# Attention stage: the pi weights of four batches on a block diagonal, spread by six products of 376 columns instead of 24 of 94

## The chip, the cores and the metric

The kernel runs on one core of a Trainium2 chip. The metric is the time of one execution in microseconds (us) as the device measures it. The engines are named as the profile names them: PE is TensorE's matmul side and PEld its weight loads, DVE is VectorE, ACT is ScalarE, POOL is GpSimd and SP is SyncE, which here only issues DMAs.

## The reference, cut to what matters

64 batches of 93 tokens (16 image patches and 77 text tokens) with 192 features go through an embedding, one attention stage and one feed-forward stage. The change is in the attention stage:

```python
w = (x @ w_qkv).reshape(b, n, h, -1).transpose(0, 2, 1, 3)        # 12 heads of 64
w_normed = w / maximum(norm over n, 1e-12)
logits = sum(w_normed * w_normed, -1) * temp
Pi = softmax(logits, axis=-1)                                      # over the 93 tokens
Pi_norm = Pi / (sum(Pi, -1) + 1e-08)
dots = einsum('bhn,bhnd->bhd', Pi_norm, w * w)[:, :, None, :]
out = -(w * Pi[..., None]) * (1 / (1 + dots))
return out.transpose(0, 2, 1, 3).reshape(b, n, -1) @ w_out + b_out
```

Everything is float32 here. For each batch and each head there is one row Pi of 93 weights. Each has to stand beside all 64 rows of its head before it can be multiplied with w, which lies with the 768 head features on the partitions.

## The kernel before, in words

The kernel has three stages. The first (to about 150 us) makes the embeddings. The second is the attention, together with the feed-forward's routing: layer norm, codes z, scores, the top four of 64 in each of eight groups, gates. The third, from about 750 us, is a long pipeline of small experts over 12 tiles.

The second stage works on 16 units of `UB` = 4 batches (372 tokens). It is a software pipeline written out by hand: in pass `i` (`pass_pe`, `pass_dve`, `pass_act`, `pass_pool`, `pass_sp`) each engine does a part of unit `a = i` (layer norm, w, squares, norms, logits, softmax), of unit `b = i - 1` (pi spread, attention, output product, residual) and of unit `g = i - 2` (second layer norm, codes, scores, gates). Each engine has one queue and runs it in the order in which those functions call; semaphores join the engines.

The softmax leaves `pi`, 128 partitions x 94: partition `32 b + h` holds batch b and head h, columns 0 to 92 the weights and column 93 the reciprocal of their sum (`pi_complete`, L1178). To spread it, `spread_pi(u, c)` (L1460 to L1469) does, for each of the `CH` = 6 chunks of 128 head features, one product per batch: the weights `headsel[:, b, c]` (128x128, ones where partition 32 b + h belongs to a feature's head) times the whole of `pi`, which gives 94 columns. The four results stand side by side in one PSUM bank of `pair0`. On DVE, `w_pi` (L1183, L1186) multiplies w with the 4 x 93 columns and copies the four scales out; on POOL, `w2_pi` (L716) multiplies with w again, and `attn_dots` (L1190) sums on DVE.

What stands around it in a pass, in the order of the queues:
- PE: `spread_pi` 0 and 1; the six transposes of unit a's normed tokens (L1413); `spread_pi` 2 and 3; six transposes of unit g (L1413 again); `spread_pi` 4 and 5; `z_product` (L1441); `w_product` 0 to 5 (L1426) with `scores` (L1449) between; the output products (L1487); `logits` (L1456); gate transposes (L1475). The two banks of `pair0` are shared: chunk c of a spread waits until `w_pi(c-2)` has read its bank (`s_rsc`).
- DVE, at the end of a pass: `logits_max` (L1220, L1222), `pi_recip` (L1162), `pi_made` (L1166), `pi_sum` (L1170), `pi_sum_eps` (L1174), `pi_complete` (L1178), the norm of the next unit (L1119), the residual (L1229, L1232), `bn_stats` (L1106). At the start of the next: `w_pi` 0, `bn_aggr` (L1112), `w_pi` 1, the norm of unit g (L1119), `w_pi` 2, 3, `attn_dots` 0, 1, `w_pi` 4, 5, `attn_dots` 2 to 5, `neg_attn` (L1197 to L1201), and then the eight-fold max and the marking of the gates (`top8` L1128, `mark` L1139).
- ACT: `logits_exp` (L901), then the gate copies 1 and 2 (L913), and in the next pass the copies of the transposed tokens (L865), w (L871), squares with a sum (L873, 93 columns each) and scores (L897).
- POOL: `rstd` (L689, L691), `w2_pi`, the shifts and products of the gates (L704, L710), `attended` (L724).

Constants are set in stage 1: `headsel` is cleared by DVE (L1009) and its ones are placed by POOL in four steps (L669); `lsel` is cleared by POOL between the stages (L683).

Of the kernel before, what the change touches and what calls it, by code (L numbers as in the profile page):

```python
# [28 lines left out]
AX = mybir.AxisListType  # L29
# [6 lines left out]
N = NI + NT  # L36
# [10 lines left out]
CH = INNER // 128  # L47
UB = 4
# [48 lines left out]
def wait(eng, sem, value):  # L97

    if isinstance(value, int) and value <= 0:
        return  # L100
    eng.wait_ge(sem, value)
# [42 lines left out]
def build(nc, t):  # L144

    with ExitStack() as ctx:
        def sem(name):
            return ctx.enter_context(nc.semaphore(name))
# [20 lines left out]
        class Carver:  # L169
# [4 lines left out]
            def __call__(self, rows, shape, dt=F32):  # L174
# [7 lines left out]
                if len(shape) > 1:  # L182
# [7 lines left out]
        pair0, pair1 = ring[:, 0:2], ring[:, 2:4]  # L190
# [43 lines left out]
        cl = Carver(LATE)  # L234
# [4 lines left out]
        bout = cl(ST, [D])  # L239
        tempc = cl(128, [1])  # L240
        maskh = cl(128, [CH, HEADS])
        headsel = cl(128, [UB, CH, 128])
        pz = cl(DH2, [2, 128])
        cbd = cl(128, [E])

# [1 line left out]
        c2 = Carver(0, LATE)  # L247
# [21 lines left out]
        pe_ = c2(128, [N])  # L269
        psm = c2(128, [1])  # L270
        prc = c2(128, [1])
        pi = c2(128, [N + 1])
        pss = c2(128, [1])
        pse = c2(128, [1])
        rsc = c2(128, [CH, UB])
# [42 lines left out]
        s_zero = sem("constants_zeroed")  # L318
# [16 lines left out]
        s_c2 = sem("attention_constants")  # L335
# [14 lines left out]
        s_pr, s_pi, s_ps, s_pse, s_pix = (sem("pi_recip"), sem("pi_made"), sem("pi_sum"), sem("pi_sum_eps"),  # L350
                                          sem("pi_complete"))
        s_pb = sem("pi_spread")
        s_wpi, s_rsc = sem("w_pi"), sem("pi_scale_copied")
        s_w2pi = sem("w2_pi")
        s_dt, s_ds, s_dm, s_na = sem("dots_summed"), sem("dots_scaled"), sem("dots_negated"), sem("neg_attn")
# [71 lines left out]
        def stage1_over(eng):  # L427

            eng.wait_ge(s_todma[0], 64 * 6)
            eng.wait_ge(s_todma[1], 64 * 5)  # L430
            eng.wait_ge(s_idma[0], 16 * 4)
            eng.wait_ge(s_idma[1], 16 * 4)
            eng.wait_ge(s_ws, 2)
            eng.wait_ge(s_bc, 1)
            eng.wait_ge(s_w2c, 1)

        def has(u):

            return not isinstance(u, int) or 0 <= u < UNITS
# [189 lines left out]
        def _(pool):  # L629
            p_ = nc.gpsimd  # L630
# [34 lines left out]
            text_rstd(1)  # L665
            gather(3, 1)
            for b in range(UB):
                v = headsel[:, b].rearrange("p c (o d) -> p c o d", o=2)
                p_.affine_select(out=v, in_=v, compare_op=ALU.not_equal, fill=1.0, base=-32 * b,  # L669
                                 pattern=[[-2, CH], [-1, 2], [0, DH]], channel_multiplier=1).then_inc(s_c2, 1)  # L670
            text_rstd(2)
# [9 lines left out]

            stage1_over(pool)
            p_.memset(lsel, 0.0)  # L683
            p_.memset(mh2, -0.5).then_inc(s_c2, 1)
            pool.wait_ge(s_c2, 7)

# [119 lines left out]
        def _(act):  # L806
            a_ = nc.scalar
# [91 lines left out]
            def logits_exp(u):  # L899
                act.wait_ge(s_lm, u + 1)  # L900
                a_.activation(pe_, lg, ACT.Exp, bias=nmax, accum_out=psm).then_inc(s_pe, 1)  # L901

            def scores_exp(u, s):
                act.wait_ge(s_sd, SUB * u + s + 1)
                wait(act, s_gu, SUB * u)
                a_.activation(se[:, s], sd[:, s], ACT.Exp).then_inc(s_se, 1)
# [9 lines left out]
            def pass_act(i):  # L916
                a, g = i, i - 2
                if has(a):
                    copy_xT("A", a)
                if has(g):  # L920
                    copy_xT("G", g)
                if has(g):
                    z_copies(g)
                for c in range(CH):
                    if has(a):
                        w_copy(a, c)
                    if has(g):
                        if c < SUB:
                            scores_copy(g, c)
                        if c == 1:  # L930
                            z_part2(g)
                            scores_exp(g, 0)
                        if c == 4:
                            scores_exp(g, 1)
                if has(g - 1):
                    copy_bias(g - 1)
                if has(g):
                    scores_exp(g, 2)
                    gates_copy(g, 0)
                if has(a):  # L940
                    logits_exp(a)
                if has(g):
                    gates_copy(g, 1)
                    gates_copy(g, 2)
# [58 lines left out]
        def _(dve):  # L1003
# [3 lines left out]
            v_.memset(cbd, 0.0)  # L1007
            v_.memset(maskh, 1.0)
            v_.memset(headsel, 0.0)  # L1009
            v_.memset(b2p[:], 0.0)  # L1010
            v_.memset(w2p[:], 0.0).then_inc(s_zero, 1)
            dve.wait_ge(s_const, 1)
# [82 lines left out]


            stage1_over(dve)
            v_.memset(sc[:, :, :, M:M + 8], SENTINEL)
            v_.memset(v4, SENTINEL).then_inc(s_c2d, 1)
            dve.wait_ge(s_c2, 7)  # L1100
# [62 lines left out]

            def pi_made(u):
                dve.wait_ge(s_pr, u + 1)
                v_.tensor_scalar(pi[:, 0:N], pe_, prc, None, ALU.mult).then_inc(s_pi, 1)  # L1166

            def pi_sum(u):
                dve.wait_ge(s_pi, u + 1)
                v_.tensor_reduce(pss, pi[:, 0:N], AX.X, ALU.add).then_inc(s_ps, 1)  # L1170

            def pi_sum_eps(u):
                dve.wait_ge(s_ps, u + 1)
# [1 line left out]

            def pi_complete(u):
                dve.wait_ge(s_pse, u + 1)
                v_.reciprocal(pi[:, N:N + 1], pse).then_inc(s_pix, 1)  # L1178

            def w_pi(u, c):  # L1180
                dve.wait_ge(s_pb, CH * u + c + 1)
# [52 lines left out]
            def pass_dve(i):  # L1234
                a, b, g = i, i - 1, i - 2
                if has(b):
                    w_pi(b, 0)
                if has(g):
                    bn_aggr("G", g)
                if has(b):  # L1240
                    w_pi(b, 1)
                if has(g):
                    for s in range(SUB):
                        norm("G", g, h1, s)
                if has(g) and not has(b):
                    v_.memset(zst[96:ZROWS], 1.0).then_inc(s_ones, 1)
                if has(b):
                    w_pi(b, 2)
                    w_pi(b, 3)
                    attn_dots(b, 0)  # L1250
                    attn_dots(b, 1)
                    w_pi(b, 4)
                    w_pi(b, 5)
                    for c in range(2, CH):
                        attn_dots(b, c)
                    neg_attn(b)

                if has(g):
                    top8(g, 0)
                    top4(g, 0)  # L1260
                    mark(g, 0)
                    top8(g, 1)
                    top4(g, 1)
                    raw(g, 0)
                    mark(g, 1)
                    raw_sum(g, 0)
                    top8(g, 2)
                    raw_recip(g, 0)
                    top4(g, 2)
                    raw(g, 1)  # L1270
                    mark(g, 2)
                if has(a):
                    norms_floored(a)
                if has(g):
                    raw_sum(g, 1)
                if has(a):
                    norms_inverted(a)
                if has(g):
                    raw_recip(g, 1)
                if has(a):  # L1280
                    head_weights(a)
                if has(g):
                    raw(g, 2)
                if has(a + 1):
                    dve.wait_ge(s_x0, 16 * (a + 2))
                    bn_stats("A", a + 1, x0)
                if has(g):
                    raw_sum(g, 2)
                if has(a + 1):
                    bn_aggr("A", a + 1)  # L1290
                if has(g):
                    raw_recip(g, 2)
                if has(a):
                    logits_max(a)
                if has(a):
                    pi_recip(a)
                    pi_made(a)
                    pi_sum(a)
                    pi_sum_eps(a)
                    pi_complete(a)  # L1300
                if has(a + 1):
                    for s in range(SUB):
                        norm("A", a + 1, x0, s)
                if has(b):
                    residual(b, 0)
                    residual(b, 1)
                if has(b):
                    dve.wait_ge(s_h1, b + 1)
                    bn_stats("G", b, h1)
# [60 lines left out]
        def _(pe):  # L1370
# [88 lines left out]

            def spread_pi(u, c):  # L1460
                pe.wait_ge(s_pix, u + 1)
                if c < 2:
                    pe.wait_ge(s_wsq, CH * u + 5 + c)
                else:
                    wait(pe, s_rsc, CH * u + c - 1)
                for b in range(UB):
                    last = t_.matmul(pair0[:, c % 2, (N + 1) * b:(N + 1) * (b + 1)], headsel[:, b, c],  # L1467
                                     pi, start=True, stop=True)
                last.then_inc(s_pb, 1)  # L1469

            def gates_transposed(u, s):
                pe.wait_ge(s_z1, u + 1)
# [218 lines left out]
```

## Time and profile before

| | us |
|---|---|
| median of three runs | 1595.14 |
| lowest and highest | 1578.29 and 1599.72 |
| the profiled execution, whole | 1585.62 |
| its span, first to last instruction | 1583.9 |
| the stretch of 14 passes of stage 2 (208.8 to 704.5 us) | 495.7 |
| mean granted TensorE clock of the span | 0.933 |

The granted clock is a share of 2.4 GHz; 0.50 is the lower level, 1.2 GHz. A row of a timeline gives start, duration, engine, line, operation, shapes, count, and in brackets the idle time of the engine before it with what ended it. A float32 product shows as two MATMUL instructions and two LDWEIGHTS, so a spread of one chunk is 8 of each.

### The profile page before, as it was taken

To read this page: it belongs to the slowest core of one execution; us is meant where nothing else is said; L and a number is where in the kernel's file an instruction comes from. 1 tells how busy PE (TensorE), PEld (TensorE's weight loads), DVE (VectorE), ACT (ScalarE), POOL (GpSimd) and SP (SyncE) were. 2 spreads that over 40 slices of the span, in tenths; PEclk is the share of its full clock that TensorE was granted. 3 is DMA by queue.
4 is the path that set the end of the run, shared out by engine and by line. 5 is a ranking of instruction groups with operands and counts; after the bars stand their busy time and mean duration, and the time that the engine had idled before them with its cause. 6 is when DMAs were issued, how large, how long until landed. Compare 5 with 4: busy or idle time off the path is not lost.

```text
span 1583.9 us, 29744 instructions
## 1 busy us (share of the span) xinstructions
PE 1408.5 (89%) x8184; PEld 644.7 (41%) x8184; DVE 1183.5 (75%) x3446; ACT 1031.2 (65%) x2119; POOL 1048.1 (66%) x770
## 2 busy tenths in 40 slices
PE   4971789989999998986699999999999999999997
PEld 2630567766666666764122222222222222222222
DVE  4573278887888978877678877777787787778874
ACT  0231344444544544432599999999999899999995
POOL 3650266566666766655487787877878778787775
PEclk9955799999999989987699999999999999999998
DMA  8436311121211211113311413214132131321310
GB/s 245 117 97 89 49 30 54 55 63 56 80 53 53 65 53 53 56 48 103 88 37 43 90 34 70 55 42 89 28 76 55 42 76 40 78 55 42 74 38 13
DMA packets 93351, 102.28 MB, mean 65 GB/s; under 512 B 12215, under 2 KB 90575, under 8 KB 93007
## 3 DMA queue, kind: packets, MB, share of 16 engines
q1 hardware_dynamic: 89945, 96.01, 24.8%
q0 software_dynamic: 2112, 3.79, 0.9%
q10 hardware_dynamic: 1232, 1.84, 0.4%
q14 instruction: 45, 0.37, 0.1%
q8 instruction: 17, 0.28, 0.1%
HBM read 64.83 MB, written 33.52 MB: 62 GB/s over the span
## 4 chain that ended last, share of the span: by engine, by line
issue 40%; PE 19%; DVE 18%; POOL 13%; DMA 4%; ACT 3%; SPq 1%; POOLq 1%; DVEq 0%; ACTq 0%
POOL arena L783 10%; DVE arena L1139 4%; PE ring L1456 3%; DVE arena L1128 3%; DMA arena<-h_scratch 3%; PE ring L1467 2%; DVE arena L1119 2%; PE ring L1426 2%; PE ring L1569 2%; PE code L1582 2%; PE ring L1441 2%; DVE arena L1214 1%; PE ring L1375 1%; DVE arena L1154 1%; PE ring L1384 1%
## 5 line engine op out<-in xcount | busy, mean ns | idle before, releaser
L1336 DVE TENSOR_TENSOR arena<-ring,arena 128x496 f32<-128x496 f32 x1008 | 614.0, 668 | 178.3 <-ACT ring L974 134.9
L783 POOL TENSOR_TENSOR arena<-arena 128x992 f32<-128x992 f32 x264 | 603.7, 2298 | 178.3 <-ACT arena L974 167.9
L1569 PE MATMUL ring<-arena,w_stack 99*128 99x496 bf16 x1536 | 401.9, 379 | 16.2 <-DVE arena L1336 15.4
L974 ACT ACTIVATE ring<-ring 128x992 f32<-128x992 f32 x396 | 385.1, 987 | 34.9 <-PE ring L1569 32.5
L1582 PE MATMUL code<-arena,w_pad 128*32 128x496 f32 x3072 | 398.7, 592 | 1.5 <-ACT arena L979 0.6
L1569 PEld LDWEIGHTS ring<-arena,w_stack 99*128 99x128 bf16 x1536 | 119.4, 97 | 450.0 <-DVE arena L1336 257.0
L974 ACT ACTIVATE arena<-ring 128x992 f32<-128x992 f32 x252 | 251.3, 997 | 11.0 <-PE ring L1569 3.1
L1426 PE MATMUL ring<-arena 96*128 96x372 f32 x384 | 145.0, 510 | 5.7 <-ACT arena L873 4.4
L1582 PEld LDWEIGHTS code<-arena,w_pad 128*32 128x32 f32 x3072 | 61.1, 108 | 138.4 <-issue 115.5
L969 ACT ACTIVATE ring<-ring 128x496 f32<-128x496 f32 x216 | 112.7, 568 | 6.1 <-PE ring L1569 4.8
L1467 PE MATMUL ring<-arena 128*128 128x94 f32 x768 | 105.0, 296 | 9.1 <-DVE arena L1178 7.6
L716 POOL TENSOR_TENSOR arena<-arena 128x372 f32<-128x372 f32 x96 | 91.8, 974 | 31.8 <-DVE arena L1183 31.4
L865 ACT COPY arena<-ring 96x744 f32<-96x744 f32 x32 | 24.8, 775 | 132.9 <-PE ring L1413 132.9
L1467 PEld LDWEIGHTS ring<-arena 128*128 128x128 f32 x768 | 100.7, 211 | 13.2 <-DVE arena L1178 8.2
L1426 PEld LDWEIGHTS ring<-arena 96*128 96x128 f32 x384 | 73.9, 200 | 76.9 <-issue 28.4
L873 ACT ACTIVATE arena<-ring 128x93 f32<-128x93 f32 x384 | 92.5, 280 | 0.0
L710 POOL TENSOR_TENSOR arena<-arena 124x512 f32<-124x512 f32 x48 | 58.6, 1221 | 50.6 <-DVE arena L1158 49.4
L1413 PE MATMUL ring<-ident,arena 124*96 124x124 f32 x192 | 31.4, 308 | 64.9 <-DVE arena L1119 64.9
L689 POOL TENSOR_SCALAR arena<-arena 124x3 f32<-124x3 f32 x32 | 7.5, 234 | 121.9 <-DVE arena L1112 121.9
L873 ACT ACTIVATION_READ_ACCUMULATOR arena<-ring 128x1 f32 x384 | 86.4, 238 | 0.0
L724 POOL TENSOR_TENSOR arena<-arena 128x372 f32<-128x372 f32 x96 | 77.9, 832 | 8.7 <-DVE arena L1201 8.7
L1139 DVE MATCH_REPLACE8 arena<-arena 124x72 f32<-124x72 f32 x384 | 78.4, 217 | 0.0
(126 smaller groups left out, 1737.1 us busy)
## 6 DMA issues: line engine op xcount, KB each, us to landing
arena<-gates SPq DMA_DIRECT2D x48, 496.0 KB, 6.7
gates<-arena SPq DMA_DIRECT2D x16, 744.0 KB, 10.0
arena<-h_scratch SPq DMA_DIRECT2D x32, 279.0 KB
arena<-z_parts SPq DMA_DIRECT2D x144, 62.0 KB, 2.2
h_scratch<-arena SPq DMA_DIRECT2D x16, 279.0 KB
z_parts<-arena SPq DMA_DIRECT2D x48, 93.0 KB, 1.7
arena<-h_scratch SPq DMA_DIRECT2D x12, 372.0 KB
out_h<-arena SPq DMA_DIRECT2D x12, 372.0 KB
```

The source lines that it names most:

```text
L716: p_.tensor_tensor(w2pi[:, c], wpi[:, c], wv[:, c], ALU.mult).then_inc(s_w2pi, 1)
L724: p_.tensor_tensor(o, o, natt[:, c].unsqueeze(2).to_broadcast([128, UB, N]), ALU.mult).then_inc(s_o, 1)
L783: p_.tensor_tensor(gated[:, quad % SPACES, j:j + 2], hid[:, POOL_DUOS.index(duo) % 2], gst[:, block // EB, j:j + 2], ALU.mult).then_inc(s_ ...
L873: last = a_.activation(wsq[:, c, N * b:N * b + N], src[:, N * b:N * b + N], ACT.Square, accum_out=n2[:, c, b:b + 1])
L969: last = a_.activation(product if to_pool is None else to_pool[:, k], product, ACT.Gelu_apprx_tanh)
L974: a_.activation(product if to_pool is None else to_pool, product, ACT.Gelu_apprx_tanh).then_inc(s_hid, 1)
L1139: last = v_.match_replace(mr[:, s, g], v4[:, s, g], sc[:, s, g], CHOSEN)
L1336: v_.tensor_tensor(gated[:, quad % SPACES, j + p], duo_bank(duo, p), gst[:, block // EB, j + p], ALU.mult).then_inc(s_gat, 1)
L1426: mm = t_.matmul(o, wq[:, h, 128 * c:128 * c + 128], xT["A"][:, h], start=(h == 0), stop=(h == 1))
L1467: last = t_.matmul(pair0[:, c % 2, (N + 1) * b:(N + 1) * (b + 1)], headsel[:, b, c], pi, start=True, stop=True)
L1569: mm = t_.matmul(duo_bank(duo, p), w1s[:, x:x + 128], zst[:, o, j + p], start=True, stop=True)
L1582: mm = t_.matmul(code_bank[32 * j:32 * j + 32, 0:TN], w2p[:, chunk(2 * j + o, eb, k)], gated[:, quad % SPACES, j], start=(quad == 0), stop ...
```

## The change

`headsel` loses its batch index: one 128x128 selector per chunk serves all four batches, with ones for every partition 32 b + h of the head. In exchange pi gets a block-diagonal form: `pis`, 128 x 4 x 94, holds batch b's rows in column block b and zeros elsewhere. One product of 376 columns per chunk then gives what four of 94 gave. New work per unit: ACT copies four blocks of 32 partitions x 93 from `pi` to `pis` (`pi_placed`), behind `logits_exp` and ahead of gate copies 1 and 2; DVE writes the four scale columns with one small multiply (`pi_scale_placed`), behind `pi_complete` and ahead of the next unit's norm. PE waits for both.

```diff
-        headsel = cl(128, [UB, CH, 128])
+        headsel = cl(128, [CH, 128])
+        unitsel = cl(128, [UB])
...
-        pi = c2(128, [N + 1])
+        pi = c2(128, [N])
+        pis = c2(128, [UB, N + 1])
+        prs = c2(128, [1])
...
             for b in range(UB):
-                v = headsel[:, b].rearrange("p c (o d) -> p c o d", o=2)
+                v = headsel.rearrange("p c (o d) -> p c o d", o=2)
+                if b > 0:
+                    pool.wait_ge(s_c2, 2 + b)
                 p_.affine_select(out=v, in_=v, compare_op=ALU.not_equal, fill=1.0, base=-32 * b,
...
             p_.memset(lsel, 0.0)
+            p_.memset(pis, 0.0)
...
+            def pi_placed(u):
+                act.wait_ge(s_pi, u + 1)
+                wait(act, s_pb, CH * u)
+                for b in range(UB):
+                    rows = slice(32 * b, 32 * b + 32)
+                    last = a_.copy(pis[rows, b, 0:N], pi[rows])
+                last.then_inc(s_pip, 1)
...
                     logits_exp(a)
+                    pi_placed(a)
...
+            v_.memset(unitsel, 0.0)
...
+            dve.wait_ge(s_zero, 1)
+            for b in range(UB):
+                v_.memset(unitsel[32 * b:32 * b + 32, b:b + 1], 1.0)
...
             def pi_made(u):
                 dve.wait_ge(s_pr, u + 1)
-                v_.tensor_scalar(pi[:, 0:N], pe_, prc, None, ALU.mult).then_inc(s_pi, 1)
+                wait(dve, s_pip, u)
+                v_.tensor_scalar(pi, pe_, prc, None, ALU.mult).then_inc(s_pi, 1)
...
-                v_.reciprocal(pi[:, N:N + 1], pse).then_inc(s_pix, 1)
+                v_.reciprocal(prs, pse).then_inc(s_prs, 1)
+
+            def pi_scale_placed(u):
+                dve.wait_ge(s_prs, u + 1)
+                wait(dve, s_pb, CH * u)
+                v_.tensor_scalar(pis[:, :, N], unitsel, prs, None, ALU.mult).then_inc(s_pix, 1)
...
                     pi_complete(a)
+                    pi_scale_placed(a)
...
             def spread_pi(u, c):
                 pe.wait_ge(s_pix, u + 1)
+                pe.wait_ge(s_pip, u + 1)
...
-                for b in range(UB):
-                    last = t_.matmul(pair0[:, c % 2, (N + 1) * b:(N + 1) * (b + 1)], headsel[:, b, c],
-                                     pi, start=True, stop=True)
-                last.then_inc(s_pb, 1)
+                t_.matmul(pair0[:, c % 2, 0:UB * (N + 1)], headsel[:, c], pis.rearrange("p b n -> p (b n)"),
+                          start=True, stop=True).then_inc(s_pb, 1)
```

## Rows read from the trace of the kernel before

**Rows 1.** The page: the span, TensorE's clock in 40 slices, the spread's two groups.
```profile
span 1583.9 us, 29744 instructions
PEclk9955799999999989987699999999999999999998
L1467 PE MATMUL ring<-arena 128*128 128x94 f32 x768 | 105.0, 296 | 9.1 <-DVE arena L1178 7.6
```
**Rows 2.** Stretches of PE, PEld, DVE, ACT, POOL busy time, clock, DMA share, GB/s.
```profile
208.80:704.50 495.70, 448.87 (x2757) 335.10 (x2758) 413.63 (x1927) 225.28 (x991) 315.52 (x348) 0.95 0.18 57
526.30:559.70 33.40, 30.38 (x199) 22.74 (x200) 29.45 (x139) 16.19 (x71) 22.65 (x26) 1.00 0.20 63
...
276.10:311.10 35.00, 31.96 (x199) 24.31 (x200) 29.58 (x139) 16.19 (x71) 22.73 (x26) 0.95 0.20 61
...
665.50:704.50 39.00, 35.41 (x199) 26.29 (x200) 29.23 (x133) 16.19 (x71) 22.73 (x26) 0.87 0.15 47
```
**Rows 3.** The chain of waits in a warm pass (start, us, what).
```profile
528.20 0.17 DVE arena L1174
528.38 0.04 DVE arena L1178
...
528.47 0.13 DVE arena L1119
...
536.34 1.76 PE ring L1467 x16
538.10 1.28 PE ring L1441 x4
```
**Rows 4.** The timeline of the same pass on PE, DVE and ACT.
```profile
526.91 0.37 ACT L901 ACTIVATE arena<-arena 128x93 f32<-128x93 f32 x1 [5.30 <-DVE arena L1222]
...
529.03 1.93 PE L1467 MATMUL ring<-arena 128*128 128x94 f32 x16
529.23 0.57 ACT L913 COPY arena<-ring 128x496 f32<-128x496 f32 x1 [1.40 <-PE ring L1475]
...
530.99 0.53 DVE L1183 TENSOR_TENSOR arena<-arena,ring 128x372 f32<-128x372 f32 x1
531.65 2.02 PE L1467 MATMUL ring<-arena 128*128 128x94 f32 x16
...
532.15 0.15 DVE L1186 COPY arena<-ring 128x4 f32<-128x4 f32 x1
...
535.50 0.84 PE L1413 MATMUL ring<-ident,arena 124*96 124x124 f32 x6 [1.83 <-DVE arena L1119]
...
542.72 1.11 DVE L1128 MAX8 arena<-arena 124x8 f32<-124x64 f32 x8 [0.75 <-ACT arena L897]
```
**Rows 5.** The chain in a pass with a fallen clock.
```profile
568.89 1.48 PE ring L1413 x6
570.37 3.37 PE ring L1467 x16
573.73 2.54 PE ring L1441 x4
```
**Rows 6.** Busy time in a pause of PE and right behind it.
```profile
566.60:568.80 2.20, 0.46 (x5) 0.29 (x3) 2.13 (x4) 0.00 (x0) 1.83 (x2) 0.93 0.23 49
568.90:578.80 9.90, 9.90 (x31) 7.62 (x32) 5.56 (x17) 1.61 (x3) 5.29 (x6) 0.50 0.41 141
```
**Rows 7.** Small ACT activates on 93 columns, from the page.
```profile
L873 ACT ACTIVATE arena<-ring 128x93 f32<-128x93 f32 x384 | 92.5, 280 | 0.0
```
**Rows 8.** Clearing and waiting at the start of stages 1 and 2.
```profile
2.30 2.62 DVE L1009 MEMSET arena<- 128x3072 f32 x1 [0.59 <-issue]
16.89 2.72 DVE L1016 TENSOR_SCALAR arena<-arena 2x4928 int32<-2x4928 int32 x1 [7.55 <-DMA arena<-in_beta]
...
134.53 0.74 POOL L683 MEMSET arena<- 128x768 f32 x1 [7.40 <-DMA h_scratch<-arena]
151.17 0.88 DVE L1106 BATCH_NORM_STATS2 arena<-arena 124x6 f32<-124x192 f32 x3 [16.17 <-DMA arena<-h_scratch]
```

More of the change, by code:

```diff
@@ L352, in build @@
         s_pb = sem("pi_spread")
+        s_prs, s_pip = sem("pi_sum_recip"), sem("pi_placed")
         s_wpi, s_rsc = sem("w_pi"), sem("pi_scale_copied")
@@ L1165, in pi_made @@
                 dve.wait_ge(s_pr, u + 1)
-                v_.tensor_scalar(pi[:, 0:N], pe_, prc, None, ALU.mult).then_inc(s_pi, 1)
+                wait(dve, s_pip, u)
+                v_.tensor_scalar(pi, pe_, prc, None, ALU.mult).then_inc(s_pi, 1)
             def pi_sum(u):
                 dve.wait_ge(s_pi, u + 1)
-                v_.tensor_reduce(pss, pi[:, 0:N], AX.X, ALU.add).then_inc(s_ps, 1)
+                v_.tensor_reduce(pss, pi, AX.X, ALU.add).then_inc(s_ps, 1)
             def pi_sum_eps(u):
```

## The prediction

> **What bounds the kernel now.** The page comes first: its row of the spread's products says 105 us of PE time in 768 instructions, all in stage 2, and its clock row shows full speed in stage 3 and dips in stage 2 [rows 1]. Stage 3 is not touched by the edit, so I looked no further there. Stage 1 sees only the constants. The question is one pass of stage 2, 16 times.
>
> Then busy time by pass. A pass without a dip of the clock lasts 33.4 us; of 14 passes seven have a mean clock below 1 and last 35.0 to 39.0 us; the 14 together take 495.7, that is 28.1 more than 14 times 33.4, or 4.0 for each of the seven [rows 2]. No engine is full in a warm pass: PE is busy 30.4 of 33.4 us and DVE 29.5. The pass is a loop of dependences, so the chain of waits is read next. It goes: logits on PE, softmax on DVE, norm and residual on DVE, norm of unit g, its transposes on PE, then the spreads of chunks 4 and 5 (1.76 us), z (1.28 us), w, the scores' copy, DVE's eight-fold max and marking, and again logits [rows 3]. So of a unit's six spreads only the last pair lies on the chain. The first two pairs lie beside DVE work: PE has spread pair 0 and 1 from 529.03 on, for 1.93 us, while `w_pi(0)` starts at 530.99 straight behind other DVE work with no idle time; and behind pair 2 and 3 PE stands idle for 1.83 us until DVE has normed unit g [rows 4].
>
> **The change part by part.**
>
> *The spread products.* A pair of chunks is 16 instructions of 94 columns now, and 4 of 376 columns afterwards. The nearest row is z, 4 instructions of 372 columns with 128-wide weights: 1.28 us warm. 376 columns make it 1.29. In the chain the pair of spreads costs 1.76 [rows 3], so the gain is 0.47 us in a warm pass. With the clock at its lower level a pair costs 3.37 and z 2.54, a gain of about 0.8 [rows 5]. Three of the 16 passes show it wholly at that level, as these rows do: 3 x 0.8 + 13 x 0.47 = 8.5 us. Pairs 0, 1 and 2, 3 become shorter by as much, at no gain: the first is covered by DVE's residual and statistics, the second ends in the pause. Only unit 0 has no such cover; I count 1 us there. Together 9.5 us. Bounds: nothing (0) if the wait only moves, and 1.93 - 1.29 = 0.64 by the timeline's length of the pair, 16 x 0.64 = 10 plus the cold extra, about 12.
>
> What comes next in the way: DVE stands idle 0.75 us for the scores before the first max [rows 4]. A gain of 0.47 fits in it, so DVE does not swallow it.
>
> *One rule on weights.* In this trace z's 4 full-width weight loads are hidden below its products, since the four take just 1.28 us [rows 3]; I take the new pair the same way. The Trainium skill, "TensorE: Matmul & The Clock Gate", section "Part 3: Packing small matmuls", says that a weight load overlaps running matmuls only if it goes to other row groups. By that rule the full-height loads of the selector would stand beside the products, and the pair would gain next to nothing; z's row does not agree with it.
>
> *The scale column on DVE.* `pi_complete` is on the chain with 0.04 us only, since the norm behind it does not wait for it: from 528.38 to the norm at 528.47 is 0.09 us. Now a second instruction waits for its result and stands before the norm. A dependent pair of such small instructions is 0.18 us apart (528.20 to 528.38) [rows 3], and behind it comes the same 0.09: the norm starts 0.18 to 0.20 us later. Everything DVE does up to the norm of unit g is in order behind it, so the chain pays in full: 16 x 0.19 = 3.0 us. Bounds 0 (never seen better than its issue) and 0.3 a pass, 5 us.
>
> *The four copies on ACT.* No row shows a copy of 32 partitions. The nearest are activates of 128x93: 280 ns each [rows 7], and logits_exp itself 0.37 [rows 4]. Four: 0.65 us if they overlap as in L873, whose 384 activates take 92.5 us busy or 0.24 each plus their tails; 1.5 us at 0.37 each. I take 1.0. They start when `pi_made` is done, 527.9, and end at 528.9, about when PE is ready for the spreads (529.03). A lateness is free up to the slack: the first spread is then done at 528.9 + 0.7 = 529.6, while `w_pi(0)` does not start before 530.99 [rows 4], so 1.3 us are free. Queued behind them on ACT are the gate copies 1 and 2. Copy 1 moves from 527.28 to 528.9; PE's next transposes into that bank come at about 530.3. Copy 2 waits for PE until 529.23 anyway [rows 4] and moves to about 529.5; SP's store of the gates follows it by as much, and z's wait for it is 8 us off. Cost 0; if the copies took 0.65 each, 2.6, it would still be below 3.
>
> *The added waits.* DVE's `pi_made` waits for copies of a unit ago, ACT and DVE for spreads of a unit ago: long done. PE's wait for `s_pip` is the one above. 0.
>
> *Constants.* Clearing the selector takes DVE 2.62 us for 3072 columns, afterwards a quarter; DVE then idles 7.55 us for DMAs, so the gain is hidden. The new clearing of `pis`, 376 columns, is half of L683's 0.74 us, and four small DVE fills cost less than 0.74 together; both lie in the 16.17 us in which DVE waits for the first tokens [rows 8]. POOL's four selector steps already run one after another. 0.
>
> Sum at an unchanged clock: -9.5 + 3.0 = -6.5 us.
>
> **TensorE's clock.** In the seven passes the clock drops from 2.4 to 1.2 GHz in or right behind the pause of PE before unit g's transposes: in 566.6 to 568.8 PE is busy for 0.46 of 2.2 us, and the 9.9 us behind it run at 0.50 [rows 6]. It falls in about half of the passes, with a pause of 1.83 us [rows 4]. The change lengthens this pause: spread 3 may start when `w_pi(1)`'s copy has ended, 532.30 + 0.19, and lasts 0.64, so PE is through at 533.1; the transposes start at 535.7. The pause becomes 2.5 us, and before spread 2 there is a new one of 0.7, as the tokens' transposes are done at 531.1 and spread 2 waits for DVE until 531.8. I expect more falls, 11 of 14 to 16. Against that the stretch behind the pause is now made of long products throughout, half as long in time, so each fall should cost less: between 1.6 (the 35.0 us pass) and 4.0 [rows 2], I take 2.9. 11 x 2.9 = 32, against 28 now: +4 to +5 us. Bounds: no fall at all, -28; 15 falls at 5 us, +47.
>
> Sum: -6.5 + 4.5 = -2 us. Against the profiled execution, 1585.62, this gives 1583.6. That execution lies 9.5 us below the median of the three runs shown, which spread by 21 us. Their mean is 1591.0, the median 1595.1. As the forecast is for a median of a few runs, I put it in between: **1588 us**. A difference of under 2% (32 us) counts as no change here.
>
> **Rivals.**
> - *The clock turns against it.* Place: the pause before unit g's transposes. It decides once nearly all passes fall and a fall is no cheaper than now: 15 x 4.0 = 60, +32; with -6.5 that is +25, 1613 us against the runs. For it: the pause of 1.83 grows to 2.5. Against: the products behind are dense. At 5 us per fall, as in the 39.0 us pass, it is 15 x 5 - 28 - 6.5 = +40: 1628, beyond 2%. Chance 0.15, of this 0.05 for the latter.
> - *The clock turns for it.* As many falls as now but each at 1.6 us, 7 x 1.6 - 28 = -17, with -6.5 gives 1565; none at all gives -34.5, 1554. For it: the shorter recovery. Against: a longer pause. Chance 0.15, of this 0.04 for none.
> - *The copies are late.* If an ACT copy of 32 partitions costs 1 us instead of 0.25, the spread starts 3 us later and DVE waits 1.8 a pass for it: 16 x 1.8 = +29 - 6.5, 1611. No row has such a cost. Chance 0.04.
> - *The product gains nothing.* If the weight loads are not hidden, four times the 0.11 us at which the 16 follow one another (1.76 / 16) come on top of 1.29, 1.73 in all, the old value. Then only the DVE cost stays: +3 + 4.5, 1595. It is what the page's rule above would do. Chance 0.04.
> - *Forecast*: a near wash, 1588, its own range 1572 to 1604. Chance 0.62.
>
> **How the numbers follow.** Beyond 2% faster (below 1556): only the case without any fall, 0.04. Beyond 2% slower (over 1620): 0.05 from the first rival, 0.01 from late copies. The rest, 0.90, is within 2%. The range 1566 to 1611 takes the forecast's own, nearly all of the first two rivals' milder halves and the fourth; what lies outside is about 2 in 10.
>
> **What the profile of the changed kernel would show.** The pair of chunks 4 and 5 in the chain with 4 instructions of 1.3 us in a warm pass; right wherever DVE's wait before the first max shrinks from 0.75 to about 0.5. The norm behind the scale column 0.2 us later after L1178's successor. A warm pass of 33.1 us instead of 33.4. PE idle 2.5 us before unit g's transposes, and more passes with a mean clock below 1. ACT's four copies over before the gate transposes end. I would be wrong if a warm pass is not shorter, if DVE waits for the first spread, or if passes with a dip become fewer.

## The result: 1.5% slower, and the profile after

Before, the median of four runs was 1589.51 us (1578.29 to 1599.72); with the change it is 1615.14 us (1609.02 to 1626.94). The ratio is 1.0146, interval [1.0098, 1.0195]. I had forecast 1588 us with a range to 1611. The time lies outside the range, by a cause that stands nowhere in my prediction. A ratio, here and below, leaves out the executions in the slow state, which take over 1.5% longer than the fastest one of their kernel.

The profiled executions differ by the same 25.6 us: spans 1583.9 and 1609.5 us. The page of the changed kernel first: the span, TensorE's clock in 40 slices, the spread's products (columns as in [rows 1]), and the instruction queue q14 with packets, MB and share. Its packets come where DVE's program needs them, at its branches above all, so it is read as DVE's.

```profile
span 1609.5 us, 28796 instructions
PEclk9855799999999998996799999999999999999998
q14 instruction: 45, 0.37, 0.1%
L1495 PE MATMUL ring<-arena 128*128 128x376 f32 x192 | 85.2, 572 | 17.1 <-DVE arena L1205 8.4
```

The spread did what the edit says: 192 instructions in 85.2 us in place of 768 in 105.0. Yet the kernel is longer. The first reading that helps is to cut both spans into the same five stretches, by the same landmarks (the first logits of stage 2, the end of its last pass, the tiles' first instructions in stage 3):

| us | before | after | difference |
|---|---|---|---|
| start, stage 1 included | 171.3 | 175.0 | +3.7 |
| stage 2, 15 passes | 530.0 | 524.3 | -5.7 |
| transition | 144.2 | 147.1 | +2.9 |
| stage 3, 11 steps from tile to tile | 723.1 | 747.7 | +24.6 |
| end | 15.4 | 15.4 | 0 |

Stage 2, where the edit is, became shorter. All but 1 us of the loss is in stage 3, whose code the edit does not touch. Next, stage 3 by tile: busy time of PE, PEld, DVE, ACT, POOL, clock, DMA share and GB/s of two tiles in a row, before

```profile
910.90:978.40 67.50, 65.15 (x396) 16.39 (x395) 52.37 (x88) 61.66 (x78) 51.47 (x23) 1.00 0.25 57
978.40:1043.90 65.50, 64.70 (x396) 16.34 (x394) 51.87 (x86) 61.50 (x78) 51.46 (x23) 1.00 0.27 58
```

and after:

```profile
911.90:985.70 73.80, 67.58 (x396) 16.65 (x395) 52.40 (x88) 61.61 (x78) 51.48 (x23) 0.95 0.23 52
985.70:1051.20 65.50, 64.66 (x396) 16.33 (x394) 51.83 (x86) 61.47 (x78) 51.48 (x23) 1.00 0.26 58
```

Tiles go in pairs, as DVE's loop holds two. One tile of a pair takes 65.5 us in both kernels. The other takes 67.5 before and 73.8 after, at a clock of 0.95. Four pairs are so, the last is not: a loop of five turns is branched back in four times. 4 x 6.3 = 25 us is the whole difference of stage 3. The work in the two tiles is the same (396 products, 78 on ACT).

What DVE does in the long tile: its timeline around the branch (start, duration, what, in brackets the idle time before it and what ended it), before

```profile
968.17 1.26 DVE L1336 TENSOR_TENSOR arena<-ring,arena 128x496 f32<-128x496 f32 x2 [0.55 <-ACT ring L974]
971.64 7.24 DVE L1336 TENSOR_TENSOR arena<-ring,arena 128x496 f32<-128x496 f32 x12 [2.21 <-issue]
```

and after, with PE's timeline beside it:

```profile
969.12 1.26 DVE L1364 TENSOR_TENSOR arena<-ring,arena 128x496 f32<-128x496 f32 x2 [0.55 <-ACT ring L991]
976.66 3.58 DVE L1364 TENSOR_TENSOR arena<-ring,arena 128x496 f32<-128x496 f32 x6 [6.28 <-issue]
...
977.39 0.59 PE L1596 MATMUL ring<-arena,w_stack 99*128 99x496 bf16 x1 [5.45 <-DVE arena L1364]
977.92 1.88 PE L1609 MATMUL code<-arena,w_pad 128*32 128x496 f32 x8
...
984.22 1.04 PE L1609 MATMUL code<-arena,w_pad 128*32 128x496 f32 x8
```

In both kernels DVE stands still behind the branch, and it waits for no other engine: the releaser is "issue". Before it is 2.21 us, after 6.28 us. PE waits 5.45 us for DVE's result, and then its clock is at its lower level: eight products of L1609 take 1.88 us at 977.92 and 1.04 us from 984.22 on. So the longer standstill costs 4.1 us directly. In the kernel before TensorE's clock stays at 1.00 through this stretch; here it is at the lower level for 6.8 us, and 4.1 us become 6.3. The waits of DVE on "issue" (us in total, times, longest) of before, and then of after, say the same in one line each:

```profile
DVE arena L1336 <- issue: 8.6, 4, 2.3
```

```profile
DVE arena L1364 <- issue: 25.8, 4, 6.7
```

### The profile page after: what moved, and what is told of

It reads as the page before. It is cut to its first block, busy times and chain, and to the rows that moved or that the text cites. A ratio compares the mean times of both kernels' runs of the same rounds, so it can differ in the third digit from the quotient of the medians.

```text
span 1609.5 us, 28796 instructions
## 1 busy us (share of the span) xinstructions
PE 1393.9 (87%) x7608; PEld 587.6 (37%) x7608; DVE 1187.0 (74%) x3467; ACT 1050.8 (65%) x2183; POOL 1049.4 (65%) x771
## 4 chain that ended last, share of the span: by engine, by line
issue 42%; DVE 18%; PE 17%; POOL 13%; DMA 4%; ACT 2%; SPq 1%; POOLq 1%; DVEq 0%; ACTq 0%
POOL arena L790 10%; DVE arena L1160 4%; PE ring L1484 3%; DVE arena L1149 3%; DMA arena<-h_scratch 3%; DVE arena L1140 2%; PE ring L1495 2%; PE ring L1596 2%; PE code L1609 2%; PE ring L1454 1%; PE ring L1403 1%; PE ring L1469 1%; PE ring L1441 1%; DVE arena L1241 1%; PE ring L1412 1%
## 5 line engine op out<-in xcount | busy, mean ns | idle before, releaser
L1609 PE MATMUL code<-arena,w_pad 128*32 128x496 f32 x3072 | 404.3, 599 | 1.6 <-ACT arena L996 0.6
L1454 PE MATMUL ring<-arena 96*128 96x372 f32 x384 | 138.5, 492 | 5.8 <-ACT arena L880 4.3
L1609 PEld LDWEIGHTS code<-arena,w_pad 128*32 128x32 f32 x3072 | 61.5, 108 | 141.3 <-issue 114.7
L1495 PE MATMUL ring<-arena 128*128 128x376 f32 x192 | 85.2, 572 | 17.1 <-DVE arena L1205 8.4
L1441 PE MATMUL ring<-ident,arena 124*96 124x124 f32 x192 | 33.5, 323 | 70.1 <-DVE arena L1140 70.1
L1514 PE MATMUL code<-arena 128*124 128x192 f32 x384 | 70.6, 335 | 3.9 <-POOL arena L731 3.9
```

Source lines behind the costliest of these rows:

```text
L1454: mm = t_.matmul(o, wq[:, h, 128 * c:128 * c + 128], xT["A"][:, h], start=(h == 0), stop=(h == 1))
L1495: t_.matmul(pair0[:, c % 2, 0:UB * (N + 1)], headsel[:, c], pis.rearrange("p b n -> p (b n)"), start=True, stop=True).then_inc(s_pb, 1)
L1609: mm = t_.matmul(code_bank[32 * j:32 * j + 32, 0:TN], w2p[:, chunk(2 * j + o, eb, k)], gated[:, quad % SPACES, j], start=(quad == 0), stop ...
```

## The experiments

The theory. The edit adds 22 instructions to DVE's program ahead of its stage 3 loop (fills of the unit selector, waits, the placing of the scale). The loop has 330 instructions; its first is number 1050 in DVE's program before and 1072 after. If DVE fetches instructions in blocks and keeps only a few, then a branch back to a block that is gone waits for a fetch, and where the loop lies against the blocks sets how long. (Numbers of instructions count from 0, register and waiting instructions included.) The rivals: the change itself disturbs stage 3 (a buffer, a semaphore, data that arrives late), or the transfers of stage 3 collide otherwise. The first runs tell them apart: the same code shifted by instructions that do nothing, and the same code without the branch. Fillers are memsets of one element that nobody reads.

**Before, shifted by 22: s1.**

```
+        spare = sb("spare", [1, 32])
...
+            for k in range(22):
+                v_.memset(spare[:, k:k + 1], 0.0)
             stage2_over(dve)
```

> The kernel before, with 22 one-element fills of an unused cell on DVE ahead of its wait for the end of stage 2, so that DVE's loop of stage 3 begins 22 instructions later in the program, as it does in the changed kernel (1072 instead of 1050); nothing else differs. Theory A (placement: DVE's fetch of instructions after the taken branch of the stage 3 loop hits a block boundary): stage 3 grows as in the changed kernel, four times 6.2 us = +25 us, about 1610; DVE's pause after each branch is 6.3 us instead of 2.2. Theory B (the change itself slows stage 3, by PSUM or SBUF traffic, data or layout): 22 x 0.06 us hidden under the wait, no change, about 1588.

Measured: 1623.09 us, ratio to before 1.0212 [1.0093, 1.0331]; stage 3 is 750.1 us. The long tile:

```profile
935.10:1009.66 74.56, 66.33 (x396) 16.52 (x394) 52.10 (x87) 61.57 (x78) 51.47 (x23) 0.95 0.22 52
```

Nothing of the change is in this kernel, and it has the changed kernel's stage 3. That alone refutes the first rival. The second, that shifted transfers collide, falls with p2 and p3 below, where two fillers more or less decide.

**After, shifted by 8 more (loop at 1080): s2.** The same edit with `range(8)`.

> The changed kernel with 8 such fills, that is with more DVE work. Theory A: the loop's first instructions, which now stand just ahead of a block boundary, move behind it; one fetch is enough, DVE's pause goes back from 6.3 to about 2.2 us and the time falls by about 25 us, to 1590. Theory B: 1615 as the changed kernel, or 0.5 us more.

Measured: 1575.96 us, 0.9934 [0.9875, 0.9993]. I expected the pause to go back to 2.2 us; it went altogether. The long tile's window, DVE's run through the branch, and its instruction queue:

```profile
904.67:970.16 65.49, 64.72 (x396) 16.38 (x394) 52.11 (x87) 61.47 (x78) 51.44 (x23) 1.00 0.25 58
...
961.92 6.08 DVE L1367 TENSOR_TENSOR arena<-ring,arena 128x496 f32<-128x496 f32 x10 [0.55 <-ACT ring L992]
...
q14 instruction: 25, 0.20, 0.0%
```

DVE fetches 25 packets where the other three kernels fetch 45: the 20 that are missing are five for each of the four branches. 0.20 MB in 25 packets is 8 KB a packet.

**After, without the branch: s3. Before, without the branch: s4.**

```
-        with dve.Fori(0, (TILES - 2) // 2) as i:
+        for i in range((TILES - 2) // 2):
```

> The changed kernel with DVE's loop of stage 3 written out (five bodies of two tiles, no taken branch). Theory A: all four pauses go, 4 x 8.3 us = 33 us less than the changed kernel, about 1582, and every tile but the last takes 65.5 us. Theory B: no change, 1615.

> The kernel before with the same loop written out. Theory A: the four pauses of 2.0 us a pair of tiles go, 8 us less than the kernel before, about 1581. The written-out changed kernel against this one then shows what the change itself does, free of placement: by the two traces stage 2 is 5.7 us shorter with it, so I expect 1582 less 6 for it, about 1575, unless the rest of stage 1 (3.7 us longer in the first trace of the changed kernel) belongs to the change; then the two are equal within 3 us.

Measured: s3 1582.79 us, 0.9967 [0.9919, 1.0015]; s4 1597.53 us, 1.0037 [0.999, 1.0085]. The standstills are gone in both, and stage 3 takes 721.5 and 721.3 us. For s3 the time is what I expected, though not by tiles of 65.5 us. For s4 I expected a gain of 8 us, and its ratio shows none: without the loop the tiles take 66.05 us or a little more, as this one of s3, 0.57 more than the 65.48 of a tile in a resident loop, and that eats most of the 2.0 us that every second tile saves. Stage 3 is 1.8 us shorter than before.

```profile
914.27:980.32 66.05, 65.14 (x396) 16.34 (x394) 52.12 (x87) 61.49 (x78) 51.47 (x23) 1.00 0.25 58
```

**Before at the same place as s2: s5** (30 fillers, loop at 1080).

> The kernel before, with 30 one-element fills on DVE behind stage 2, so that its loop of stage 3 begins at instruction 1080, as in the changed kernel with 8 fills, where the pauses had gone. Placement theory: every tile but the last 65.5 us, 8 us less in stage 3 than the kernel before. Against the changed kernel at the same place it shows the change by itself: stage 2 longer by the mean of what the traces so far show, 540 against 523, so this one about 17 us slower than the changed kernel with 8 fills. Rival (stage 2 is unchanged on the mean, the differences are chance): equal within 5 us.

Measured: 1582.06 us, 0.9888 [0.9829, 0.9946], the placement's own gain for the kernel before. Stage 3 is 715.5 us, as in s2.

```profile
916.49:981.99 65.50, 64.73 (x396) 16.39 (x394) 52.11 (x87) 61.47 (x78) 51.47 (x23) 1.00 0.26 58
```

I had expected it 17 us behind s2. The medians lie 6.1 apart, but they do not come from one chip; the pair r1, r2 below compares on one.

**Where the block ends: p2 (loop at 1074), p3 (1076).** The changed kernel with 2 and with 4 fillers.

> The changed kernel with 2 fills: DVE's loop of stage 3 begins at instruction 1074. In the changed kernel (1072) DVE runs three instructions behind the taken branch, 1072 to 1074, and then stands for 4.3 us; so a block of instructions should begin at 1075. Placement theory: one instruction is left in the old block, the pause stays near 6 us and each second tile at 73 to 74 us. Rival (any fill removes the pause, because it shifts the timing of stage 3): 65.5 us.

> The changed kernel with 4 fills: the loop begins at 1076, just behind the boundary that the traces point to, and ends at 1405. Placement theory: it then touches three blocks of 128 instructions instead of four, nothing has to be fetched again and all tiles but the last take 65.5 us, as with 8 fills. Rival (it needs the larger distance of 8 fills): 67 to 74 us in each second tile.

Measured, one run each: p2 1616.45 us, p3 1573.11 us. Two instructions lie between them. Stage 3 is 748.2 and 715.3 us, 33 of the 43 us; most of the rest is the stretch ahead of stage 2, 183.8 and 170.8, of which more at r2. A branch tile of p2

```profile
916.49:990.60 74.11, 67.89 (x396) 16.70 (x395) 52.36 (x88) 61.61 (x77) 51.45 (x23) 0.95 0.23 52
...
981.28 3.00 DVE L1367 TENSOR_TENSOR arena<-ring,arena 128x496 f32<-128x496 f32 x5 [6.29 <-issue]
```

and the same of p3:

```profile
906.47:971.95 65.48, 64.71 (x396) 16.38 (x394) 52.03 (x87) 61.48 (x78) 51.53 (x23) 1.00 0.26 58
```

All places together: 1050 pauses 2.21 us; 1072 and 1074, 6.3 us; 1076 and 1080, nothing.

**The change by itself: r1 (after, loop at 1080) and r2 (before, loop at 1080)**, 12 runs each on the same chip.

> The changed kernel with 8 fills once more, beside the kernel before at the same place of the loop. With placement out of the way, what is left is the change in stage 2. Clock theory: with a fall of the clock as frequent but shorter it is 6 to 12 us faster than the kernel before with 30 fills, about 1576. Rival (only the 0.16 us of a warm pass): 2 to 3 us faster.

> The kernel before with 30 fills, loop at 1080. Clock theory: about 1585, 6 to 12 us above the changed kernel at the same place, and about 8 us below the kernel before. Rival: within 3 us of the changed kernel.

Measured: r1 1579.51 us (1570.93 to 1584.17), 0.9923 [0.9886, 0.996]; r2 1587.99 us (1577.08 to 1596.93), 0.9999 [0.9962, 1.0036]. Stage 3 is 715.3 us in both. So at equal placement the change is 8.5 us faster, 0.5%. s3 and s4, again a pair of one chip, gave 14.7. The two profiled executions do not show where the gain lies: r1's stage 2 took 527.6 us and r2's 520.7. One execution of each is too few for it, as stage 2 scatters by more.

By its ratio r2 did not beat the kernel before, though its stage 3 is 7.8 us shorter. Its median is 7.0 us below the 1595.04 of all 23 executions of the kernel before beside it, and 3.9 below the 1591.89 of the 16 that the ratio keeps, so these runs do not settle whether the 7.8 us show in full. In r2's profiled execution the stretch ahead of stage 2 took 182.6 us against 171.3, and over all traces that stretch varies from 170.0 to 185.2. It goes with TensorE's clock: the mean granted clock of the stretch is 0.74 in the three shortest (170.0 to 171.3: t1, p3, before) and 0.69 to 0.70 in the three longest (182.6 to 185.2: r2, p2, s5), both spreads among each. Why it differs is open.

**Where the change's gain is: w1 (after, loop at 1080) and w2 (before, loop at 1080), with products in the pauses.** Before unit g's transposes PE gets three (w1) or two (w2) products with the spread's weights, into a bank that is free; they keep it busy and compute nothing that is read.

```
             spread_pi(b, 3)
+            if has(b) and has(g):
+                for k in range(3):
+                    t_.matmul(pair1[:, 0, 0:UT], headsel[:, 0], wsq[:, k], start=True, stop=True)
```

> The changed kernel with 8 fills, and with three products of 372 columns into a free bank in PE's pause behind spread 3 (their results are never read). Clock theory (what a pass takes above 33.2 us is TensorE's clock that falls in this pause): the clock stays at 2.4 GHz in nearly all passes, stage 2 goes from 518 to about 500, the time from 1576 to about 1558. Rival (the excess has another cause, or the three products, 1.9 us in a pause of 2.2, delay unit g's transposes): no gain, or up to 5 us slower.

> The kernel before with 30 fills and two such products in its pause of 1.8 us. Clock theory: the same floor, 33.4 us a pass, stage 2 from about 540 to 503; the change would then be worth only its 0.16 us a pass, 3 us, against the changed kernel with warm products, where without them it is worth 17. Rival (the change gains through shorter DVE or ACT work): the gap between the two stays 17 us.

Measured: w1 1560.55 us, 0.9742 [0.9681, 0.9804]; w2 1562.03 us, 0.9785 [0.9719, 0.9852]. These two are the fastest versions; the kernel before took 1594.69 us beside them, so both are over 30 us faster than it, and more against the changed one. The 14 passes of stage 2 are at full clock, w1 first, then w2:

```profile
211.17:687.46 476.29, 436.15 (x2337) 287.26 (x2336) 419.34 (x1938) 243.12 (x1047) 315.38 (x349) 1.00 0.19 59
```

```profile
206.47:676.34 469.87, 442.05 (x2813) 325.52 (x2813) 413.12 (x1924) 224.96 (x991) 315.84 (x349) 1.00 0.19 60
```

Stage 2 took 503.1 us in w2, as expected, and 510.4 in w1 where I expected about 500 (more on that at the end). With the clock kept up the change is worth 1.5 us by the medians, nothing that these runs can tell from zero. The pair is not a clean one: twelve of w1's passes and three of w2's are of a second, longer kind (at the end), whatever the spread. A warm pass by itself is 0.16 us shorter with the change, 2.6 us in 16. That the rest of the 8.5 us of r1 against r2 is the clock is argued from these figures, not measured by itself.

**The scale column alone: t1.** The changed kernel with 19 fillers (loop at 1080), the scale column left at zero.

```
-                v_.reciprocal(prs, pse).then_inc(s_prs, 1)
+                v_.reciprocal(prs, pse).then_inc(s_pix, 1)
...
-                    pi_scale_placed(a)
```

> The changed kernel without the placing of the scale column (the fourth-power of the sum's reciprocal never reaches the selector product, its column stays zero), with 19 fills so that the loop of stage 3 stands at 1080 too. By the trace of the changed kernel the placing delays the next norm by 0.24 us: a pass without a fallen clock goes from 33.24 to 33.00 us. Rival (the delay is hidden elsewhere): 33.24 as before.

In that text a phrase about a fourth power of the sum's reciprocal is a slip; the reciprocal of the sum is meant. Measured, one run: 1564.46 us. A warm pass takes 33.00 us where the changed kernel takes 33.24: the added DVE step costs 0.24 us a pass. That is 4 us in 16; the rest of its distance to r1 is not explained by the step, and it is one execution on another chip, with four falls of the clock in the 14 passes where r1's trace has eleven.

## Why the prediction was wrong, point by point

**Stage 3: the step that failed.** It is in the first paragraph: "Stage 3 is not touched by the edit, so I looked no further there." The text of stage 3 is not touched, but its place in DVE's program is, by the 22 instructions ahead of it, and that was worth +24.6 us of the 25.6. The last step of the list, the constants and the added waits, priced those instructions at 0, by their time alone; the runs show +24.6 us in its place. The trace of before had a sign of it: four waits of 2.2 us on "issue" in stage 3, and tiles of 65.5 and 67.5 us in turn. I had not asked what a wait for nothing is. None of my rivals had it either; that the one called "the clock turns against it" gives 1613 us is a coincidence, for there the loss was to be in stage 2. That the time stayed within 2%, to which I gave 0.90, is luck too: no term of mine held it there, and place alone moves this kernel's stage 3 by 33 us (p2 against p3), more than 2%.

How it works, as far as runs show it: a loop of 330 instructions costs nothing if it starts at 1076 or 1080. If it starts at 1050, 1072 or 1074, DVE stands still in each taken branch, and five more packets a branch are fetched. Behind the branch the loop that starts at 1072 runs three instructions (of registers, which the timeline leaves out; in the trace they start at 972.12, 972.25 and 972.36), and then DVE stands another 4.3 us until 976.66. The loop of p2, which starts at 1074, runs one (976.84) and stands until 981.06. So both stop ahead of instruction 1075: a border of blocks lies between 1074 and 1075, a loop that begins ahead of it lies in one block too many, and the block behind the border is not there.

The packets' own times show the rest. In the changed kernel's turn they start at 970.2, 974.4 and 977.7 us, and DVE goes on 1.9 us after the first and 2.3 us after the second; the last two of the five come alone, at 1031.9 and 1085.0. Before, they start at 969.3, 975.1 and 979.1: DVE goes on 2.0 us after the first, and the second comes while it works on the 25 instructions from 1050 to 1074, so only one fetch is waited for. That is the difference of 2.2 and 6.3 us. For starts between 1050 and 1072 the pause was not tried.

The Trainium skill, "Runtime: NRT & Kernel Launch", section "Instruction fetch mechanics", says that a taken branch to a target outside the pages now held makes the engine fetch the target page before it goes on, and that two pages of 256 instructions are held. The traces agree on the stall and put 2.2 and 6.3 us on it. With the border at 1075 the page's grain fits the five places: 330 instructions lie in two pages from 1076 on and in three from 1050, 1072 or 1074. Blocks half as long fit as well, and the packets speak for them. The two lone packets are 53 us apart, in which this loop runs about 130 of its instructions, and straight code (s3) takes some 850 instructions more than a program with the loop and fetches seven packets more, 32 in place of 25: one packet of 8 KB for 128 instructions or so. In a stalled turn five are fetched: the four blocks of 128 that the loop touches, and one ahead. In s2, whose loop touches three, one packet comes at 941.4 and none until 1513.1, so the three and the one ahead are all held. Four blocks of 128 are as much as the page's two of 256. What stays open is whether a loop's place is judged by 128 or by 256, as no second border was tried.

**The spread pair on the chain: right.** In a warm pass and in one with a fallen clock the changed kernel's chain reads (start, us, what; L1441 is unit g's transposes here, L1495 the spread pair, L1469 z):

```profile
397.97 0.84 PE ring L1441 x6
398.81 1.27 PE ring L1495 x4
400.08 1.25 PE ring L1469 x4
...
325.18 1.47 PE ring L1441 x6
326.65 2.51 PE ring L1495 x4
329.16 2.35 PE ring L1469 x4
```

1.27 in place of 1.76 us, 2.51 in place of 3.37 [rows 3, 5]: gains of 0.49 and 0.86, forecast 0.47 and 0.8. The pair of 376 columns follows z's rows of before, 1.28 and 2.54 us, to three hundredths, and in the warm pass its second two weight loads (PEld, 0.47 us from 399.01) lie inside its products (1.43 us from 398.65 in the timeline), so the full-height loads are hidden. The rule of the Trainium skill that I set against it, and the rival built on it, are refuted here.

**The scale column: right in kind, a little dearer.** 

```profile
390.61 0.17 DVE arena L1200
390.81 0.03 DVE arena L1205
390.84 0.10 issue
390.94 0.07 DVE arena L1140
```

From L1200 to the norm it is 0.33 us, before 0.09 [rows 3]: +0.24, forecast 0.19. t1 gives the same 0.24 as a whole pass.

**The copies, the pauses: right.** The timeline of the same pass:

```profile
390.14 1.10 ACT L916 COPY arena<-arena 32x93 f32<-32x93 f32 x4 [0.54 <-DVE arena L1188]
390.81 0.23 DVE L1205 TENSOR_SCALAR arena<-arena 128x4 f32<-128x4 f32 x1
391.26 1.05 ACT L929 COPY arena<-ring 128x496 f32<-128x496 f32 x2
391.49 1.52 PE L1495 MATMUL ring<-arena 128*128 128x376 f32 x4
393.46 0.53 DVE L1210 TENSOR_TENSOR arena<-arena,ring 128x372 f32<-128x372 f32 x1
394.12 1.62 PE L1495 MATMUL ring<-arena 128*128 128x376 f32 x4 [0.47 <-DVE arena L1213]
...
397.97 0.84 PE L1441 MATMUL ring<-ident,arena 124*96 124x124 f32 x6 [2.24 <-DVE arena L1140]
```

Four copies in 1.10 us (forecast 1.0), over before the first spread starts, which does not wait for them; cost 0. The pause before unit g's transposes is 2.24 us (forecast 2.5, before 1.83), the new one 0.47 (forecast 0.7). A warm pass is 33.2 us (forecast 33.1, before 33.4).

**TensorE's clock: right in that each fall gets cheaper, wrong in the sum's sign.** Windows of the 14 passes, and of a pass with a dear fall, a cheap one and none:

```profile
209.97:699.30 489.33, 425.37 (x2254) 281.57 (x2253) 417.91 (x1938) 242.75 (x1047) 315.09 (x349) 0.96 0.18 58
...
312.50:349.60 37.10, 32.39 (x162) 21.21 (x162) 30.00 (x140) 17.44 (x75) 22.55 (x25) 0.91 0.18 56
349.60:385.30 35.70, 30.91 (x162) 20.48 (x162) 30.68 (x140) 17.45 (x75) 22.54 (x25) 0.95 0.19 59
385.30:418.50 33.20, 29.26 (x162) 19.44 (x162) 29.25 (x140) 17.46 (x75) 22.64 (x25) 1.00 0.20 63
```

The longer pause brought eight falls in 14 passes, before seven; I had 11. Each is cheaper, as I said: a pass with one is 2.4 to 3.9 us above a warm one, before up to 5.6, and no stretch at the lower level is longer than 6.8 us where before had 10.2. Over the traces the number scatters, from 3 to 11 with the old spread (before, s1, s4, s5, r2: 35 in all) and from 5 to 11 with the new (after, s2, s3, p2, p3, r1: 49 in all), but a fall lasts 7.3 us on the mean with the old and 4.6 with the new. That falls would rise by half, 7 to 11, is borne out by neither count. The excess over warm passes is 489.3 - 14 x 33.24 = 24.0 us, before 28.1 [rows 2]: -4 where I had put +4 to +5. By eight falls that is 3.0 us each, forecast 2.9, so of this term it is the number of falls that was mis-sized. Not all of either is the clock: nine of these passes, and before five, are of the second kind (last section), at some 0.9 us each, which leaves nearer 16 us for the clock, and before 23 to 24. Per trace this scatters more than it differs. In the 15 passes from the first logits on, the kernels with the old spread and a loop (before, s1, s5, r2) took 520.7 to 547.6 us, those with the new one (after, s2, p2, p3, r1) 518.1 to 527.6. The worst is gone rather than the best better. That falls are shorter because the chain behind the pause has less to do in them is what I had argued; the cold pair's 0.86 us is the part of it that a row shows.

**Sum.** At equal placement I had -2 us for the change; the pairs show -8.5 and -14.7. Without the 24.6 us of stage 3 the time would have been 1590.5, well inside the range; they took it out. One term more stands in no part of my list: the transition between the stages is 147.1 to 147.7 us in the looped kernels with the new spread and 144.2 to 145.1 in those with the old, a loss of some 3 us that w1 alone (143.6) does not have. Its cause was not looked for.

## What to carry to other kernels

An instruction that is added ahead of a loop moves that loop in its engine's program, and a loop that just fits what the engine holds of its code, here 330 instructions, can then cost microseconds in each turn. Look in the profile for waits with the releaser "issue" that come once per turn, and for stretches that alternate in length with equal work; before the worth of an edit is judged, put its loops at the same place in both versions, with fillers or with a pair of shifted runs. A pause on one engine must be priced with the clock of TensorE behind it: 4.1 us of standstill became 6.3 here, and two products a pass in a pause of PE were worth 20 us in the kernel before (s5 to w2, one chip), over twice the change.

## What the runs showed that I had not expected

- Straight code is not free here: DVE's stage 3 without a branch takes 66.05 us a tile, in a resident loop 65.48.
- Stage 2 has a second kind of pass, 0.93 us longer at full clock, in the kernel before (33.40 and 34.33 us), after (33.24 and 34.17) and t1 (33.00 and 33.93). In such passes DVE's L1148 of the kernel before takes 1.61 instead of 0.68 us, with the same shape:

```profile
438.52 1.61 DVE L1148 SCALAR_TENSOR_TENSOR arena<-arena 124x512 f32<-124x512 f32 x1
...
547.21 0.68 DVE L1148 SCALAR_TENSOR_TENSOR arena<-arena 124x512 f32<-124x512 f32 x1
```

  POOL's L704 starts beside it in both cases, within 0.02 us, and one of the two engines pays:

```profile
438.52 1.06 POOL L704 TENSOR_TENSOR arena<-arena 124x512 f32<-124x512 f32 x1
...
547.22 1.59 POOL L704 TENSOR_TENSOR arena<-arena 124x512 f32<-124x512 f32 x1
```

  Where the two start together, every trace has just these two pairs: DVE 1.61 and POOL 1.06 us, or DVE 0.68 and POOL 1.59. DVE is on the chain, and its 0.93 us are the pass's. So these two instructions do not run freely side by side; which of them goes first, and with it the kind of the pass, stays open. w1 is made up almost wholly of such passes (476.29 / 14 = 34.0 us), w2 has few (469.87 / 14 = 33.56), which is how the one missed and the other met its expectation.
